# Expert tiles that carry their tokens' numbers and write finished tokens straight to the output

## The reference, cut to what matters

```
mod = (silu(c) @ wmod).reshape(2, 6, 1, 256)          # sa, ca, ga, sb, cb, gb, one row per batch
ga, gb = sign(g) * max(|g|, 0.25)                     # sign(0) counts as +1
h = layernorm(x) * (1 + ca) + sa
x = x + ga * attention(h)
h = layernorm(x) * (1 + cb) + sb
top = argmax(h @ gate_w.T + gate_b + expert_bias)     # one expert for each token
y[token] = relu(h[token] @ w1[top] + b1[top]) @ w2[top] + b2[top]
out = x + gb * y
```

## Time and profile before

| | |
|---|---|
| time, median of 3 runs | 1976.83 us (1970.1 to 1981.98) |
| the profiled execution's own time | 1973.19 us |
| its span, first to last instruction | 1971.4 us |
| PE busy | 1810.6 us, 92% of the span |
| DVE busy | 1672.1 us, 85% |
| ACT busy | 1377.2 us, 70% |
| POOL busy | 597.1 us, 30% |
| moved by DMA | 199.82 MB, mean 101 GB/s |

### The profile page before, as it was taken

One profiled execution on the slowest core, in us unless ns is written; L12 is line 12 of the kernel. 1 busy time (PEld: TensorE's weight loads), 2 busy tenths in 40 slices (PEclk: granted clock), 3 DMA queues, 4 the chain that ended last, 5 costly groups with the idle time before them and its releaser, 6 DMA issues. The chain is left out here.

```text
span 1971.4 us, 39432 instructions
## 1 busy us (share of the span) xinstructions
PE 1810.6 (92%) x15410; PEld 909.0 (46%) x15410; DVE 1672.1 (85%) x1838; ACT 1377.2 (70%) x2504; POOL 597.1 (30%) x396
## 2 busy tenths in 40 slices
PE   7976999999999999999999999999999658999990
PEld 4532333333333333333333333333333647999990
DVE  6778899999999999999999999999965546777774
ACT  1321788888888888888888888888886225666640
POOL 1125211261151233116115123311820243343426
PEclk8985899999999999999999999999999858999995
DMA  5865011421231142142124115211143316777745
GB/s 187 237 161 106 32 57 45 77 75 49 71 80 45 60 94 66 44 77 66 55 70 84 44 49 105 66 45 45 47 146 95 94 62 198 224 224 224 224 147 176
DMA packets 141169, 199.82 MB, mean 101 GB/s; under 512 B 40976, under 2 KB 88368, under 8 KB 139216
## 3 DMA queue, kind: packets, MB, share of 16 engines
q1 hardware_dynamic: 126848, 172.83, 30.9%
q0 software_dynamic: 3552, 10.36, 2.1%
q10 hardware_dynamic: 10608, 14.42, 2.1%
HBM read 115.23 MB, written 67.13 MB: 92 GB/s over the span
## 5 line engine op out<-in xcount | busy, mean ns | idle before, releaser
L1222 DVE TENSOR_REDUCE att_mx<-att_PM 128x2 f32<-128x1024 f32 x1024 | 1245.2, 1225 | 71.0 <-PE att_PM L1079 64.1
L1190 ACT ACTIVATE att_probs<-att_PS 128x512 f32<-128x512 f32 x2048 | 1112.0, 596 | 191.4 <-PE att_PS L1066 152.5
L1112 PE MATMUL att_PV<-att_probs,att_VU 128*32 128x256 f32 x8192 | 656.1, 392 | 7.8 <-ACT keep_sums L1211 6.2
L1066 PE MATMUL att_PS<-att_QE,K 50*128 50x512 f32 x2048 | 534.5, 498 | 1.9 <-ACT att_probs L1190 1.8
L1079 PE MATMUL att_PM<-K,QM 50*128 50x512 f32 x2048 | 438.4, 413 | 23.7 <-DVE att_mx L1222 15.0
L1066 PEld LDWEIGHTS att_PS<-att_QE,K 50*128 50x128 f32 x2048 | 202.8, 184 | 433.7 <-ACT att_probs L1190 412.5
L1112 PEld LDWEIGHTS att_PV<-att_probs,att_VU 128*32 128x32 f32 x8192 | 162.7, 108 | 369.1 <-issue 201.5
L956 POOL CAST att_mh<-att_m 128x16 fp32r<-128x16 f32 x32 | 6.3, 196 | 808.3 <-DVE att_m L1229 808.3
L1079 PEld LDWEIGHTS att_PM<-K,QM 50*128 50x128 f32 x2048 | 206.1, 191 | 46.1 <-DVE att_mx L1222 36.5
L571 POOL TENSOR_TENSOR QM<-QS,QM 16x1024 fp32r<-16x1024 f32 x62 | 146.6, 2364 | 8.5 <-POOL QM L972 6.1
L562 POOL TENSOR_TENSOR K<-KS,K 16x4096 fp32r<-16x4096 f32 x14 | 125.2, 8944 | 1.8 <-POOL K L983 1.3
(11 more groups left out here) (216 smaller groups left out, 1571.9 us busy)
## 6 DMA issues: line engine op xcount, KB each, us to landing
H<-in_w SPq DMA_DIRECT2D x44, 1024.0 KB, 5.5
routed_rows<-att_zero SPq DMA_DIRECT2D x32, 1024.0 KB, 4.3
att_QE<-QM SPq DMA_DIRECT2D x32, 512.0 KB, 3.1
QS<-qkT SPq DMA_DIRECT2D x186, 64.0 KB, 2.4
KS<-qkT SPq DMA_DIRECT2D x42, 256.0 KB, 9.3
qkT<-KS ACTq DMA_DIRECT2D x16, 512.0 KB, 5.7
KS<-routed_rows SPq DMA_DIRECT2D x23, 256.0 KB, 2.8
expert_rows<-QS ACTq DMA_DIRECT2D x23, 256.0 KB, 5.2
```

The source lines that it names most:

```text
L1066: nc.tensor.matmul(PS[score_bank(i)][:], K[r % BODY // CHUNKS][rows, ab, kt * P:(kt + 1) * P], QE[r % 2][rows, ab, :], start=True, stop=Tr ...
L1112: last = nc.tensor.matmul(PV[32 * h:32 * h + VW, cols], VU[r // CHUNKS % 2][:, j, h, :], probs[:, j % SLOTS, h, cols], start=j == 0 and ha ...
L1190: nc.scalar.activation(probs[:, kt % SLOTS, h, :], PS[score_bank(i)][:], ACT.Exp).then_inc(exps, 1)
L1222: nc.vector.reduce_max(mx[:, r % 2, at:at + 2, kc], PM[bank][:], AX).then_inc(maxima, 1)
```

## The change: what it does

- **Rows with numbers.** A row of `g.hs` has RW = 258 elements: 256 values, then the token's number as an integer, then one unused. `number_rows` copies the numbers into `g.H2`'s rows, once for each of the 8 lots. Rows that no token writes are filled with 1.0 instead of 0.0. As an integer that is above 4095, so the indirect DMAs' bound skips such rows.
- **x and gate in DRAM.** A new tensor `g.x2` holds 512 numbers for each token: x and gb. gb is written by SP in the second to last step of attention (`spread_gates`, 2 DMAs of 2 MB), x by SP in the tail (8 DMAs of 512 KB, each after its lot's additions).
- **Tail.** The six operations for `g.result` go.
- **Experts.** The loop is written out. Raw weights have two buffers, rows four. POOL's program for tile k is: gather x and gate of the 256 tokens (two indirect DMAs, `fetch`), send tile k - 1 to the output (two indirect DMAs, `send`), then the low part of w1 of tile k + 1 (`split`). DVE's bias addition becomes `finish`, three operations in a chain. ACT's store goes.
- **Combine** goes.

```
-            nc.vector.tensor_copy(g.blk[:], table[:, 1, :])
...
-            nc.vector.tensor_copy(g.result[:], slotf[:]).then_inc(small, 1)
+            nc.vector.tensor_copy(g.blk[:], table[:, 1, :]).then_inc(small, 1)
...
+            def spread_gates():
+
+                hold(gating, GATED)
+                for b in range(B):
+                    sp.dma_start(g.x2[b * N:(b + 1) * N, D:2 * D].rearrange("(t p) d -> p t d", p=P),
+                                 g.mod[:, b, 3:4, :].to_broadcast([P, TB, D])).then_inc(g.x2_in, 16)
...
+                if last and r == BODY - 2:
+                    spread_gates()
...
+            for i in range(LOTS):
+                sp.wait_ge(added, 2 * i + 2)
+                sp.dma_start(g.x2[i * CH:(i + 1) * CH, 0:D].rearrange("(t p) d -> p t d", p=P), g.X[:, lot(i), :]
+                             ).then_inc(g.x2_in, 16)
...
+            def fetch(k):
+
+                pool.wait_ge(in_rows[k % RING], 16 * (k // RING + 1))
+                if k >= 2:
+                    pool.wait_ge(y_ready, (k - 1))
+                for n in range(SUB):
+                    nc.gpsimd.indirect_dma_start(tokens[k % 2][:, n, :], None, g.x2,
+                                                 bass.IndirectOffsetOnAxis(numbers[k % RING][:, n, :], 0),
+                                                 bounds_check=B * N - 1, oob_is_err=False).then_inc(fetched[k % 2], 16)
+
+            def send(k):
+                pool.wait_ge(y_ready, k + 1)
+                for n in range(SUB):
+                    nc.gpsimd.indirect_dma_start(out_rows, bass.IndirectOffsetOnAxis(numbers[k % RING][:, n, :], 0),
+                                                 y[k % 2][:, n, :], None,
+                                                 bounds_check=B * N - 1, oob_is_err=False).then_inc(sent[k % 2], 16)
+
+            def split(k):
+                if k == 1:
+                    pool.wait_ge(w1_lo, PIECES)
                 for c in range(PIECES):
                     pool.wait_ge(w1_hi, PIECES * k + c + 1)
...
+                    if k >= 2:
+                        pool.wait_ge(layer1, KF * (k - 1))
+                    nc.gpsimd.tensor_tensor(piece(w1_part[k % 2][1], c), piece(w1[k % 2], c),
+                                            piece(w1_part[k % 2][0], c).bitcast(F32), ALU.subtract).then_inc(w1_lo, 1)
...
+            for k in range(NT):
+                fetch(k)
+                if there(k - 1):
+                    send(k - 1)
+                if there(k + 1):
+                    split(k + 1)
+            send(NT - 1)
...
+            def finish(k):
+
+                par = k % 2
+                dve.wait_ge(in_b2[par], 16 * (k // 2 + 1))
+                dve.wait_ge(layer2, k + 1)
+                if k >= 2:
+                    dve.wait_ge(sent[par], 16 * SUB * (k // 2))
                 nc.vector.tensor_add(y[par], psy[par][:], b2[par][:].unsqueeze(1).to_broadcast([P, SUB, D])
-                                     ).then_inc(y_ready, 1)
...
+                                     ).then_inc(summed, 1)
+                dve.wait_ge(summed, k + 1)
+                dve.wait_ge(fetched[par], 16 * SUB * (k // 2 + 1))
+                nc.vector.tensor_mul(y[par], y[par], tokens[par][:, :, D:2 * D]).then_inc(gated, 1)
+                dve.wait_ge(gated, k + 1)
+                nc.vector.tensor_add(y[par], y[par], tokens[par][:, :, 0:D]).then_inc(y_ready, 1)
```

More of the change, by code:

```diff
@@ L37 @@
 PIECES = 2
+RW = D + 2
+HEADS_AT = 64
+FILL_PART = 544
+FILLS = 4
 class Ctx:
@@ L1798, in store @@
-            def store(k, par):
-                act.wait_ge(y_ready, k + 1 + AHEAD)
-                act.sem_inc(g.tick_act)
-                act.dma_start(g.ys.rearrange("(k s p) d -> k p s d", s=SUB, p=P)[bass.ds(k, 1)]
-                              .rearrange("o p s d -> p (o s) d"), y[par]).then_inc(stored[par], 16)
-            act.sem_inc(hidden, AHEAD * KF)
-            for par in range(2):
-                act.sem_inc(stored[par], 16)
-            copy_turned(0, 0)
-            act.wait_ge(g.scattered, 16 * T)
@@ L1809, in _, with copy_turned @@
-            first_weights(1, 1)
-            def tile(k, par, i):
-                act.wait_ge(in_b1[par], 16 * (i + 1))
+                    nc.scalar.copy(piece(w2_part[k % 2][0], c), piece(w2[k % 2], c)).then_inc(w2_hi, 1)
+            def copy_turned(k):
+                act.wait_ge(turned, k + 1)
+                nc.scalar.copy(hT[k % 2][0], pst[k % 2][:]).then_inc(hT_hi, 1)
+            copy_turned(0)
+            first_weights(1)
+            for k in range(NT):
+                par = k % 2
+                act.wait_ge(in_b1[par], 16 * (k // 2 + 1))
@@ L1820, in tile @@
-                if there(k, -1):
-                    store(k - 1, 1 - par)
-                if there(k, 1):
-                    second_weights(k + 1, 1 - par)
-                if there(k, 2):
-                    first_weights(k + 2, par)
-            over_tiles(act, tile)
-            store(NT - 1, (NT - 1) % 2)
-            for par in range(2):
-                act.wait_ge(stored[par], 16 * ((NT + 1 - par) // 2) + 16)
+                if there(k + 1):
+                    copy_turned(k + 1)
+                    second_weights(k + 1)
@@ L1862, in _ @@
                                         ALU.subtract).then_inc(w1_lo, 1)
-            low_weights(0, 0)
-            low_rows(0, 0)
-            def tile(k, par, i):
-                if there(k, -1):
-                    add_bias(k - 1, 1 - par, i + par)
+            low_rows(0)
+            low_weights(0)
+            for k in range(NT):
+                if there(k - 1):
+                    finish(k - 1)
                 for p in range(HPAIRS):
                     two = slice(2 * p, 2 * p + 2)
-                    dve.wait_ge(hidden, KF * k + 2 * p + 2 + AHEAD * KF)
+                    dve.wait_ge(hidden, KF * k + 2 * p + 2)
                     nc.vector.tensor_copy(hid_part[0][:, two, :], hid[:, two, :]).then_inc(hid_hi, 1)
@@ L1876, in tile @@
                                             hid_part[0][:, two, :].bitcast(F32), ALU.subtract).then_inc(hid_lo, 1)
-                if there(k, 1):
-                    low_rows(k + 1, 1 - par)
-                    low_weights(k + 1, 1 - par)
-            over_tiles(dve, tile)
-            add_bias(NT - 1, (NT - 1) % 2, (NT + 1) // 2)
+                if there(k + 1):
+                    low_rows(k + 1)
+                    low_weights(k + 1)
+            finish(NT - 1)
         @block.tensor
@@ L1978, in build @@
      g.wmod) = ins
-    g.rope, g.row = consts
+    g.rope, g.row, g.tokens = consts
     g.out = out
@@ L2037, in build @@
             experts(nc, g)
-        combine(nc, g)
 def rope_tables():
@@ L2079 @@
     consts = []
-    for name, a in (("rope", rope_tables()), ("row", routing_row())):
+    for name, a in (("rope", rope_tables()), ("row", routing_row()), ("tokens", token_numbers())):
         arrays["const_" + name] = a
```

271 lines of the change are left out of this document (114 added, 157 removed).

## The result

| | before | changed |
|---|---|---|
| median of 4 runs | 1975.03 us | 2062.59 us (2055.03 to 2067.15) |
| ratio, 95% interval | 1 | 1.0437 [1.0412, 1.0462] |
| the profiled execution's span | 1971.4 us | 2065.1 us |
| DVE busy | 1672.1 us | 1758.6 us |
| PE's granted clock, mean | 0.946 | 0.928 |

The changed kernel is slower by 4.4%. The forecast was 2020 us in a range of 1950 to 2048. The sign and the place of the loss were right, the size was 43 us short, and the time lies 15 us above the range.

A forecast was written before the change was run, and what follows sets the result against it. The prediction took PE to pace the experts' stage at 12.26 us a tile. The span 1971.4 - 41 (combine) + 87 (21 experts' tiles) = 2017, plus 1.8 around it, made 2019, stated as 2020 us, range 1950 to 2048.

The forecast's parts named there:

- Experts, POOL and DVE: Experts: the split, behind the send, falls on DVE's third and fourth pairs; 16.4 us a tile, 87 us over 21 tiles.
- T: Start of PE's layer 1 of tile k in the experts; times within a tile count from it in us.
- the sum: Whole kernel: span 1971.4 - 41 + 87 = 2017 us, plus 1.8 around it = 2019.
- Where the stall ends: Experts: PE starts the fourth pair at T + 11.85 to 12.35, the next tile at 15.7 instead of 12.26 us.
- The clock: Experts: PE's clock drops after the gap, costing 0 to 1.7 us a tile; 0.7 taken, as idle time has two parts.
- Combine's gain: End of the kernel: 50.2 us from the last bias addition's start become 8.8, a gain of 41 us.
- about 0.5 to close: End of the kernel: what remains after the last send's landing, about 0.5 of the 8.8 us.
- Attention and tail at 0: Before the experts: attention costs 0, at most 5 us if the cover fails; tail 0, between -1 and +3.
- No stall: Rival, experts: PE keeps 12.26 us a tile and combine's gain comes in full, about 1932 us; chance 0.11.
- Behind the last pair: Rival, experts: the split slips behind the last pair, tile 13.9 or about 13 us, time 1945 to 1968; chance 0.17.
- Transfers late too: Rival, experts: gathers and scatters delay weight loads, 17.6 us or more a tile, 2045 us and above; chance 0.06.
- The second raw buffers at 0: Experts: two raw weight buffers end ACT's wait of 2.46 us for w1, off PE's path, gain 0.

The follow-up runs named there:

- e1: The changed kernel with POOL's order made fetch, split, send instead of fetch, send, split: 1956.5 us, 0.9897 of the kernel before.
- e2: The changed kernel, order kept, without the two subtractions of each split (w1's low part not computed from the second expert tile on): 1925.6 us.
- e3: The changed kernel without POOL's gathers and all sends but the last, the split made to wait for the third pair's hidden values: 2029.4 us.
- e4: The changed kernel with 28 more matmuls in layer 2 of tiles 3 to 21, filling PE's gap: 2035.3 us.
- e7: The changed kernel, order kept, with each of POOL's two subtractions written as two of half the columns: 2063.1 us.
- e11: The changed kernel with each send but the last replaced by two POOL memsets in a scratch buffer: 2076.2 us.
- e10: e9 with a POOL drain put behind the send of the second to last tile: 1920.9 us, 0.9724 of the kernel before.
- e8: The kernel before with w1's low part made by DVE at the end of its program for a tile: 1986.7 us.
- e6: The changed kernel with POOL's split waiting for the low parts of all the tile's hidden pairs: 1984.0 us, 1.0036 of the kernel before.
- e9: e5 with SP starting the load of w1 a tile earlier: 1929.0 us, 0.9762 of the kernel before.
- e5: The changed kernel with the two subtractions for w1's low part moved from POOL to the end of DVE's program for a tile: 1942.7 us.

## Why the prediction had the cause and the place right, and the size short

- **Experts, POOL and DVE: cause and place right.** The split was to start at about T + 5.5, because the send stands ahead of it; it starts at T + 5.8 to 6.0. (The terms given for the send end at T + 5.45 to 5.67, not at 5.2; the sum used 5.5, so nothing hangs on it.) It was to hold DVE's work on the pairs in all 21 tiles, and PE was to wait 65 to 90 us for low parts; PE waited 86.1. e1 shows that the order does it, e2 that without POOL's subtractions there is no hold beside the same indirect DMAs, and e3 that a late split costs nearly as much without them.
- **Where the stall ends: 0.6 to 0.9 us a tile too early.** I let two DVE instructions stand, one for each of POOL's, so that PE would get through the third pair and be back at T + 11.85 to 12.35 with 3.6 us to go. This step failed. In the trace one instruction, the third pair's cast, stands for both, and the fourth pair is not held. PE is back at T + 11.63 but with 36 of layer 2's 48 matmuls before it: 4.66 us at full clock by e4's trace (1787.50 to 1792.16). That is T + 16.3 instead of 15.7; the mean tile of e4, all at full clock, is 16.56. e3, with no indirect DMA ahead of the split, is the case that I had priced: PE is back there at T + 11.9, with the fourth pair and half 1 to go. In the changed kernel and in e7 a cast that comes beside the second send waits for everything queued behind it, in e3 and most tiles of e11 for one instruction. Why POOL's queue is let through in the one case is not known.
- **The clock: 0.6 to 0.9 us a tile too little.** I took 0.7 of a possible 1.7 since the idle time was to come in two parts. This step failed too, and for more than one reason. The idle time came in one part of 3.8 to 4.2 us; of 17.87 us a tile 1.6 are above the 16.3, and e4, which takes the gap away, got back 1.3. But two parts would not have made it cheap: in e3 the idle time does come in two, and the one tile without the half clock was 1.6 to 1.9 us shorter than the others. The full 1.7 was the better choice in either case.
- **Both together.** The stall and the clock are 1.5 us a tile: 16.4 was forecast, 17.87 measured, and 17.6 was the upper bound. (By the sum's own terms 15.4 to 17.6 a tile make 1998 to 2044 us, not 1996 to 2048.) With 21 tiles, and 12.26 for 12.31 us before, that is 30 of the missing 48 us of span (2065.1 against the 2017 of the sum). Combine gives 5 more and the later start 13, both below.
- **Combine's gain: 36 instead of 41.** The end was to take 8.8 us from the last bias addition, and took 14.3 (2050.8 to 2065.1). The step that failed is "about 0.5 to close": POOL's drain takes 7.57 us there, and e10, which moves it, ends 7.4 us sooner behind tile 22's start. In the kernel before, combine's gathers have a drain too, but it ended at 1969.1, beside DVE's and SP's last work, and showed in no row.
- **Attention and tail at 0: not settled, at most some 5 us.** Layer 1 of the first tile starts at 1633.0 in the kernel before and 1635.9 in e8, which has the same stages ahead. In the eleven profiles that have the changed kernel's attention and tail it starts between 1633.2 and 1646.3, in the mean at 1638.8. So of the 13.0 us in the two profiles shown about 4 may be the change's, and the rest is scatter between executions, which I saw as a PE clock that rises later in the first 230 us (0.76 against 0.81 on the mean there), in code that is the same. The forecast's -1 to +3 for the tail is not contradicted.
- **The rivals.** "No stall" fell. "Behind the last pair" is e6: its tile was priced at 13 us and takes 14.40, since I had left out that the split then meets DVE's subtractions for w2. The kernel would have been level with before, not faster. "Transfers late too" is not what happened: with a DMA share of 0.52 the transfers had more room than before, and e9 carries half as much again a second.
- **The second raw buffers at 0.** Nothing speaks against it in the changed kernel: ACT's waits for w1 fell from 35.2 to 13.2 us over the stage, and neither was on PE's path. For e5 against e8 it was probably wrong (see e8), which no run shows by itself.

## What to carry to other kernels

Before work is put ahead of an instruction in an engine's program, ask what the instruction will then fall upon: here no engine was full, and 5.0 of the 5.6 us that a tile lost came from two calls in the wrong order. Where POOL and DVE meet in SBUF, look at when POOL's instruction starts, not at how busy POOL is; moving the work to the busier engine was faster. And an engine that is 99% busy may still be held back (12.3 us a tile against 11.75): taking the suspect out once, as in e2, shows how much. A clock that falls after a gap is priced best from a run in which the gap is filled (e4), not by how the idle time is cut up.

## What the runs showed of the hardware

- A DVE cast issued while the second of two POOL indirect DMAs runs, with subtractions queued behind it, waits for all of them: two of 2.4 us (5.70) or four of 1.2 (5.98). Behind another subtraction it gets in after one (e3), behind two memsets in most tiles too; in three of 21 it stood through both (3.2 us, e11). The indirect DMA alone doesn't hold it: beside the first send (1793.09), and in the last tile, where nothing is queued behind the same send, the cast took 0.43 us. Why is open.
- POOL's drain after the experts' indirect DMAs takes longer the more there were since the last drain: 7.57 us after 92 (the same in the eight profiles that have 92), 3.97 after 48 (e11), 0.22 after two (e3), 0.21 after two (e10). That is 0.05 us and 0.082 for each. The one put in e10 has 90 before it and ends 7.4 us after the last of them (1908.35 to 1915.76). Elsewhere the rule is rough. After the tail's 32 scatters the drain ends 2.8 to 3.2 us behind the last (1622.8 to 1625.6 in the kernel before), where it gives 2.7, and after combine's 32 gathers 3.6 (1965.5 to 1969.1).
- An indirect DMA on POOL took 1.99 us instead of 1.05 when DVE's subtractions for w2 ran beside it (e1, 1756.77). What counts is which began first: in all 87 cases from tile 1 on (e1, e5, e6, e9, e10) in which such a subtraction was already running, it took 1.85 to 2.06 us; in the 18 of e9 and e10 in which the DMA began first, 1.01.
